# A Mamba-2 mixer with a routed low-rank FFN on one core: B/C convolution sums in two buffers, with one tap by ScalarE and GpSimd

## The reference

```
proj = xn @ in_proj_w.T            # gate, hBC, dt: 8192 + (8192 + 2*8*128) + 128 columns
hBC  = silu(causal_conv4(hBC) + conv_b)        # four taps along the tokens, per channel
dt   = softplus(dt + dt_bias);  A_dt = -exp(A_log) * dt
hs, B, C = split(hBC)              # 128 heads of 64; B and C: 8 groups of 128
Y_diag = ((C B^T) * exp(segsum(A_dt))) (hs*dt)     # inside chunks of 128 tokens
Y_off  = C @ (state carried over chunks) * exp(cumsum(A_dt))
y   = (Y_diag + Y_off + D*hs) * silu(gate), RMS-normalised over 8 groups of channels
out = x + y @ out_proj_w.T + (xn @ W.T + b) + lora_of_the_routed_rank(xn)
```

## Time and profile before

| | |
|---|---|
| median of 3 runs | 1671.41 us (1670.61 to 1672.05) |
| the profiled execution | 1669.55 us |
| its span, first to last instruction | 1667.8 us |
| TensorE matmuls busy | 1619.9 us (97%) |
| VectorE busy | 1387.0 us (83%) |
| ScalarE busy | 1262.7 us (76%) |
| GpSimd busy | 1149.4 us (69%) |
| mean granted TensorE clock | 0.994 |

### The profile page before, as it was taken

How to read it: one execution, slowest core, us unless ns; L and a number is a source line. 1 busy time by engine, 2 the same in 40 slices (tenths; PEclk the granted TensorE clock), 3 DMA queues, 4 the chain that set the end, 5 groups by cost and what they waited for, 6 DMA issues and landing times.

```text
span 1667.8 us, 28969 instructions
## 1 busy us (share of the span) xinstructions
PE 1619.9 (97%) x9662; PEld 1358.2 (81%) x9662; DVE 1387.0 (83%) x2342; ACT 1262.7 (76%) x2489; POOL 1149.4 (69%) x1472
## 2 busy tenths in 40 slices
PE   8889999999999999999997899999999999999998
PEld 6678888888888888888776788888888888888886
DVE  6778888888888888888887788888888888888887
ACT  3458888888888887888734687888888888888784
POOL 4227786777777677768652386877786777777684
PEclk9999999999999999999999999999999999999999
DMA  5134444444444444444312344444344444444431
GB/s 168 51 121 136 134 124 143 142 126 133 145 127 130 146 129 130 142 142 120 126 38 97 128 144 135 123 144 142 128 132 146 124 131 146 131 134 137 141 115 61
DMA packets 82309, 212.18 MB, mean 127 GB/s; under 512 B 11121, under 2 KB 27505, under 8 KB 81905
## 3 DMA queue, kind: packets, MB, share of 16 engines
q1 hardware_dynamic: 82160, 210.33, 40.2%
HBM read 207.14 MB, written 3.15 MB: 126 GB/s over the span
## 4 chain that ended last, share of the span: by engine, by line
PE 87%; DVE 8%; POOL 1%; issue 1%; ACT 1%; DMA 0%; POOLq 0%; DVEq 0%; ACTq 0%
PE bg L613 21%; PE bo L759 20%; PE bh L613 11%; PE bt L613 11%; PE by L812 8%; PE bg L832 5%; DVE cv L856 3%; PE bh L804 3%; PE bt L804 2%; PE bh L820 2%; PE bt L820 2%; ACT cv L319 1%; PE bo L670 1%; PE bg L738 1%; DVE ct L872 1%
## 5 line engine op out<-in xcount | busy, mean ns | idle before, releaser
L508 POOL TENSOR_TENSOR wl<-raw,wh 128x256 fp32r<-128x256 f32 x584 | 425.4, 760 | 138.4 <-ACT wh L315 138.4
L575 POOL TENSOR_TENSOR xl<-xg,xh 128x256 fp32r<-128x256 f32 x254 | 290.3, 1164 | 332.2 <-ACT xh L431 331.5
L332 ACT ACTIVATE mt<-cs_row,cs_tok 128x128 f32<-128x128 f32 x1024 | 324.8, 391 | 0.0
L589 POOL TENSOR_TENSOR wol<-raw_o,woh 128x256 fp32r<-128x256 f32 x256 | 181.6, 731 | 31.0 <-ACT woh L465 31.0
L1086 DVE TENSOR_TENSOR mt<-mt,gt 128x1024 f32<-128x1024 f32 x128 | 202.1, 1579 | 0.4 <-ACT mt L474 0.4
L759 PE MATMUL bo<-woh,xh 128*128 128x512 f32 x512 | 201.0, 393 | 0.9 <-POOL xl L575 0.9
L759 PE MATMUL bo<-wol,xh 128*128 128x512 f32 x512 | 200.4, 391 | 0.0
L759 PE MATMUL bo<-woh,xl 128*128 128x512 f32 x512 | 199.9, 391 | 0.0
L582 POOL TENSOR_TENSOR sqa<-sqa,sq 128x256 f32<-128x256 f32 x222 | 159.4, 738 | 0.9 <-ACT sq L448 0.9
L315 ACT ACTIVATE wh<-raw 128x1024 fp32r<-128x1024 f32 (+1 forms) x146 | 152.0, 1041 | 1.0 <-DMA raw<-in_w_dtag 1.0
L431 ACT ACTIVATE xh<-xg 128x512 fp32r<-128x512 f32 x128 | 81.0, 633 | 92.6 <-DVE xg L1066 92.6
(11 more groups left out here) (189 smaller groups left out, 3592.4 us busy)
## 6 DMA issues: line engine op xcount, KB each, us to landing
raw<-in_w_step SPq DMA_DIRECT2D x128, 512.0 KB, 3.5
cs_row<-cs_rows SPq DMA_DIRECT2D x128, 512.0 KB, 5.4
raw_o<-in_w_out SPq DMA_DIRECT2D x128, 256.0 KB, 4.1
ec_row<-ec_rows SPq DMA_DIRECT2D x256, 96.0 KB, 4.7
raw<-in_w_bc SPq DMA_DIRECT2D x16, 512.0 KB, 3.5
acc<-in_x SPq DMA_DIRECT2D x4, 512.0 KB, 5.7
cs_row<-in_w_ffn SPq DMA_DIRECT2D x2, 1024.0 KB, 6.8
out_dram<-acc SPq DMA_DIRECT2D x1, 1024.0 KB, 6.5
```

The source lines that it names most:

```text
L332: e = act.activation(mt[:, m % 2, h, chunk(j)], cs_row[:, m % 2, h, chunk(j)], ACT.Relu, bias=cs_tok[:, j, 2 * m + h:2 * m + h + 1], scale ...
L508: e = pool.tensor_tensor(wl[:, n % 2, cols], raw[:, n % 2, cols], wh[:, n % 2, cols].bitcast(F32), ALU.subtract)
L575: e = pool.tensor_tensor(xl[:, u, cols], xg[:, u, cols], xh[:, u, cols].bitcast(F32), ALU.subtract)
L589: e = pool.tensor_tensor(wol[:, 1 - u, cols], raw_o[:, 1 - u, cols], woh[:, 1 - u, cols].bitcast(F32), ALU.subtract)
```

## The change

It has four parts.

1. In the B/C stage the sums lie in two sets of buffers: `cv` for even groups, `sq` and `sqa` (free at that time) for odd ones (`conv_bc`). So the last tap of a group waits for the SiLU of two groups before.
2. Of the three taps that VectorE added, one goes to ScalarE and GpSimd: ScalarE writes the scaled, unshifted sum into `tap2[u]` (`two_taps`), and GpSimd adds it, shifted by one token, in two pieces of 256 and 255 columns (`add_tap`). VectorE adds the two others (`far_taps`) behind GpSimd's. In GpSimd's list the two `add_tap` of a group stand ahead of the low part of group `g + 2`, and all of them ahead of that of step 0.
3. VectorE masks the scores of group `g - 3` at the head of a group instead of between the taps of B and C, and waits for `scaled` only behind `soft_log` and `route`.
4. In the last batch's iteration m = 64 ScalarE's three instructions on the output weights and the copy of the last state stand ahead of `xh` and the square.

```diff
+        tap2 = mt[:, 0, 0], mt[:, 1, 1]
+        def conv_bc(g, u):
+            return cv[:, u, :] if g % 2 == 0 else (sq, sqa)[u]
...
+            def first_tap(b, g, u, src):
+                un = b * UNITS + 2 * g + u
+                if g != 1:
+                    act.wait_ge(v_h2, did(un - 2 if g == 0 else un - 4))
+                elif u == 0:
+                    act.wait_ge(p_sqa, squares(b - 1, STEPS - 1))
+                else:
+                    act.wait_ge(t_ss, did(b * GROUPS - 1))
+                act.activation(conv_bc(g, u)[:, :], src[:, :], ACT.Identity, bias=par_sb[:, un % UNITS, TAPS:TAPS + 1],
+                               scale=par_sb[:, un % UNITS, TAPS - 1:TAPS]).then_inc(a_tap, 1)
+            def two_taps(b, g, u, src):
+                un = b * UNITS + 2 * g + u
+                first_tap(b, g, u, src)
+                if g > 0:
+                    act.wait_ge(p_cv, did(bc_unit(b, g - 1, u)))
+                act.activation(tap2[u], src[:, :], ACT.Identity,
+                               scale=par_sb[:, un % UNITS, TAPS - 2:TAPS - 1]).then_inc(a_t2, 1)
...
-                    last_tap(b * UNITS + 2 * g, 0, bank_b[g % 2])
+                    two_taps(b, g, 0, bank_b[g % 2])
...
-                    last_tap(b * UNITS + 2 * g + 1, 1, bank_c[g % 2])
+                    two_taps(b, g, 1, bank_c[g % 2])
...
+                    ahead = m == STEPS and b + 1 == NB
+                    if ahead:
+                        weights_and_state()
                     if has(m - 2):
                         act.wait_ge(v_xg, did(n - 2))
...
-                    if has(m - 1):
-                        act.wait_ge(ld_rawo[1 - u], landed(n - 1))
...
+                    if has(m - 1) and not ahead:
+                        weights_and_state()
...
+            def add_tap(b, g, u):
+                pool.wait_ge(a_t2, did(bc_unit(b, g, u)))
+                for cols in (slice(1, 257), slice(257, L)):
+                    e = pool.tensor_tensor(conv_bc(g, u)[:, cols], conv_bc(g, u)[:, cols],
+                                           tap2[u][:, cols.start - 1:cols.stop - 1], ALU.add)
+                e.then_inc(p_cv, 1)
...
-                for g in range(2, GROUPS):
-                    split_lo(bc(b, g))
+                for g in range(GROUPS):
+                    for u in range(2):
+                        add_tap(b, g, u)
+                    if g + 2 < GROUPS:
+                        split_lo(bc(b, g + 2))
...
-                for k in range(1, TAPS):
-                    if k == 1:
-                        dve.wait_ge(a_tap, did(un))
+                for k in (2, 3):
+                    if k == 2:
+                        dve.wait_ge(p_cv, did(q))
...
-                    dve.wait_ge(scaled, SCALED)
                 soft_log(b)
                 route(b)
+                dve.wait_ge(scaled, SCALED)
                 for g in range(GROUPS):
                     un = b * UNITS + 2 * g
-                    taps_bc(b, g, 0, bank_b[g % 2])
-                    if g >= 1:
-                        silu_conv(un - 1, 1, bank_c[(g - 1) % 2], ct[:, g - 1, :])
                     if g >= 3:
                         mask_scores(b, g - 3)
-                    taps_bc(b, g, 1, bank_c[g % 2])
+                    far_taps(b, g, 0, bank_b[g % 2])
+                    if g >= 1:
+                        silu_conv(un - 1, conv_bc(g - 1, 1), bank_c[(g - 1) % 2], ct[:, g - 1, :])
+                    far_taps(b, g, 1, bank_c[g % 2])
```

More of the change, by code:

```diff
@@ L155, in mixer_kernel @@
         bank_b, bank_c, bank_t, bank_s = (bh, bt), (bg, by), (bh, bg), (bh, bt)
-        v_bc = sem("v_bc")
+        a_t2, p_cv, v_bc = sem("a_t2"), sem("p_cv"), sem("v_bc")
         ld_hp, ld_par, ld_wb, const_ok, scaled = (sem(n) for n in ("ld_hp", "ld_par", "ld_wb", "const_ok", "scaled"))
@@ L308, in _ @@
         def _(act):
-            start(act, (a_dr, a_tap, a_th, a_tg, a_rl, a_ex, a_s1, a_xh, a_sq, a_wh, a_wn, a_woh, a_bt))
+            start(act, (a_t2, a_dr, a_tap, a_th, a_tg, a_rl, a_ex, a_s1, a_xh, a_sq, a_wh, a_wn, a_woh, a_bt))
             act.wait_ge(ld_hp, 16)
@@ L324, in tanh_conv @@
                 act.activation(dst[:, :], cv[:, u, :], ACT.Tanh, scale=0.5).then_inc(a_th, 1)
+            def first_tap(b, g, u, src):
[15 more added lines that the diff above has]
+                               scale=par_sb[:, un % UNITS, TAPS - 2:TAPS - 1]).then_inc(a_t2, 1)
             def tanh_bc(b, g, u, dst):
-                act.wait_ge(v_bc, did(bc_unit(b, g, u), 3))
-                act.activation(dst[:, :], cv[:, u, :], ACT.Tanh, scale=0.5).then_inc(a_th, 1)
+                act.wait_ge(v_bc, did(bc_unit(b, g, u), 2))
+                act.activation(dst[:, :], conv_bc(g, u)[:, :], ACT.Tanh, scale=0.5).then_inc(a_th, 1)
             def rises(b, m, h):
@@ L427, in _, with weights_and_state @@
                         dt_parts(b + 1)
+                    def weights_and_state():
+                        act.wait_ge(ld_rawo[1 - u], landed(n - 1))
+                        act.activation(raw_o[:, 1 - u, :], raw_o[:, 1 - u, :], ACT.Identity,
+                                       scale=par_sb[:, 2 * GROUPS + m - 1, 6:7]).then_inc(a_wn, 1)
+                        act.wait_ge(a_wn, did(n - 1))
+                        act.wait_ge(t_out, did(n - 3))
+                        act.activation(woh[:, 1 - u, :], raw_o[:, 1 - u, :], ACT.Copy).then_inc(a_woh, 1)
+                        act.wait_ge(t_st, did(n - 1))
+                        act.wait_ge(t_off, did(n - 2))
+                        act.activation(S[:, 0, :], other[:, 0:P], ACT.Copy).then_inc(a_s1, 1)
+                    ahead = m == STEPS and b + 1 == NB
+                    if ahead:
+                        weights_and_state()
                     if has(m - 2):
@@ L480, in _ @@
         def _(pool):
-            start(pool, (p_acc, p_wl, p_wol, p_xl, p_sqa, p_rr))
+            start(pool, (p_cv, p_acc, p_wl, p_wol, p_xl, p_sqa, p_rr))
             pool.memset(ident[:, :], 0.0).then_inc(const_ok, 1)
@@ L847, in _, with far_taps @@
             start(dve, (v_bc, v_tap, v_h2, v_x, v_xd, v_m, v_s, v_y1, v_off, v_add, v_xg, v_sg, v_g, v_ms, v_acc))
-            def taps_bc(b, g, u, src):
+            def far_taps(b, g, u, src):
                 q, un = bc_unit(b, g, u), b * UNITS + 2 * g + u
-                for k in range(1, TAPS):
-                    if k == 1:
-                        dve.wait_ge(a_tap, did(un))
-                    else:
[L855 to L858, removed]
+                for k in (2, 3):
+                    if k == 2:
+                        dve.wait_ge(p_cv, did(q))
+                    else:
+                        dve.wait_ge(v_bc, did(q, 2, 1))
+                    dve.scalar_tensor_tensor(out=conv_bc(g, u)[:, k:], in0=src[:, 0:L - k],
+                                             scalar=par_sb[:, un % UNITS, TAPS - 1 - k:TAPS - k],
+                                             in1=conv_bc(g, u)[:, k:], op0=ALU.mult, op1=ALU.add).then_inc(v_bc, 1)
             def tap(n, un, u, src, k):
@@ L868, in tap, with silu_conv @@
                                          op0=ALU.mult, op1=ALU.add).then_inc(v_tap, 1)
-            def silu_conv(un, u, src, dst):
+            def silu_conv(un, conv, src, dst):
                 dve.wait_ge(a_th, did(un))
-                dve.scalar_tensor_tensor(out=dst, in0=src[:, :], scalar=1.0, in1=cv[:, u, :],
+                dve.scalar_tensor_tensor(out=dst, in0=src[:, :], scalar=1.0, in1=conv[:, :],
                                          op0=ALU.add, op1=ALU.mult).then_inc(v_h2, 1)
@@ L1027, in _ @@
                     dve.wait_ge(const_ok, CONST)
-                    dve.wait_ge(scaled, SCALED)
                 soft_log(b)
                 route(b)
+                dve.wait_ge(scaled, SCALED)
                 for g in range(GROUPS):
                     un = b * UNITS + 2 * g
-                    taps_bc(b, g, 0, bank_b[g % 2])
-                    if g >= 1:
-                        silu_conv(un - 1, 1, bank_c[(g - 1) % 2], ct[:, g - 1, :])
                     if g >= 3:
                         mask_scores(b, g - 3)
-                    taps_bc(b, g, 1, bank_c[g % 2])
+                    far_taps(b, g, 0, bank_b[g % 2])
+                    if g >= 1:
+                        silu_conv(un - 1, conv_bc(g - 1, 1), bank_c[(g - 1) % 2], ct[:, g - 1, :])
+                    far_taps(b, g, 1, bank_c[g % 2])
                     if g >= 2:
                         dve.wait_ge(t_bt, did(b * GROUPS + g - 2))
-                    silu_conv(un, 0, bank_b[g % 2], h2[:, g % 2, :])
+                    silu_conv(un, conv_bc(g, 0), bank_b[g % 2], h2[:, g % 2, :])
                     if g == 1:
@@ L1046, in _ @@
                         decays_to_end(b)
-                silu_conv(b * UNITS + 2 * GROUPS - 1, 1, bank_c[(GROUPS - 1) % 2], ct[:, GROUPS - 1, :])
```

(3 more changed lines are left out.)

## The result

| | before | after |
|---|---|---|
| median of 4 runs each, us | 1671.01 | 1648.24 (1646.76 to 1649.77) |
| ratio | | 0.9863, 95% interval 0.9846 to 0.9880 |
| profiled execution's span, us | 1667.8 | 1646.2 |
| VectorE busy, us | 1387.0 | 1367.2 |
| ScalarE busy, us | 1262.7 | 1281.6 |

The kernel is 1.4% faster: 22.9 us by the ratio, 21.6 by the two spans. The forecast was 20.9 us.

What follows compares the result with a forecast made beforehand. TensorE, busy 97% of the span, was taken as the bound, so only its waits and slow clock could pay. Gains of 10.3 (batch 0), 7.9 (batch 1) and 2.7 (end) sum to 20.9 us: 1650.5 us, range 1645 to 1656.5.

Steps and rivals of the forecast that it cites:

- The walk of batch 0: Batch 0's B/C stage, traced from router to step 0: transposes at 37.6, scores of group 1 at 59.1, step 0 at 94.3.
- the stand before step 0: Once per batch TensorE waits 4.8 us for step 0's low half, queued on GpSimd behind the last tap of C.
- slow clock in step 0 of batch 0: TensorE's clock falls behind the 4.8 us wait before step 0, charged 2.7 us; the same charge in batch 1.
- small waits of steps 0 and 1, batch 0: A TensorE wait of 0.37 us in step 0 goes because VectorE has caught up: 0.4 us gained.
- batch 1, step 0 earlier still by: Batch 1's step 0 starts at 919.4 instead of 929.56, 10.2 us earlier, before 2.7 is charged for the clock.
- the end: In the tail, copying the last state first lets VectorE go on at 1651.5 instead of 1654.24: 2.7 us gained.
- The router beside GpSimd: In batch 0 the router's tiny instructions, now beside GpSimd's first taps and a split, cost 2.7 us more.
- B: Rival: clock doesn't fall behind the 4.8 wait before step 0, or that wait is mostly hidden; 5.4 more gained, 1645.1; chance 0.10.
- C: Rival: GpSimd's adds cost about 1.16 each, or the clock falls at 37.6 too; 5.4 less gained, 1655.9; chance 0.17.
- D: Rival: GpSimd bounds the B/C stage at about 1.2 us a piece, period 9.6; slower, 1677; chance 0.04.
- GpSimd off the path: In the B/C stage GpSimd's 5.7 us a period stays below TensorE's 6.78, so its slower add costs nothing.
- VectorE's 4.8 us a period: In the B/C stage VectorE, with one tap less per sum, needs 4.8 us a period, below TensorE's 6.78.

## Why the prediction was right

**The walk of batch 0 held.** Forecast: router's transposes at 37.6, C of group 3 at 56.4, scores of group 1 at 59.1, step 0 at 94.3. Measured 37.19, 56.42, 59.27 and 93.58. The router was 0.4 early and the walk from it to the scores of group 1 took 22.1 for 21.5, which nearly cancel. The periods are 6.7 (forecast 6.78), and the stand before step 0 is 4.45 (4.8) in both batches. The tap by ScalarE takes 0.68, as forecast, and GpSimd's adds 1.41 to 1.44 a pair against the 1.48 taken from the steps' sums. The pairs beside VectorE's decays take up to 2.45; they delayed nothing.

**Part by part, by the starts of TensorE's instructions:**

| | forecast | measured |
|---|---|---|
| batch 0, step 0 earlier by | 12.6 | 106.89 - 93.58 = 13.3 |
| slow clock in step 0 of batch 0 | -2.7 | 4.45 - 2.84 for 12 matmuls = -1.6 |
| small waits of steps 0 and 1, batch 0 | +0.4 | +0.6 |
| between the B/C stages | 0 | -2.0 |
| batch 1, step 0 earlier still by | 10.2 | 10.6 |
| slow clock in step 0 of batch 1 | -2.7 | 5.15 - 2.84 = -2.3 |
| small waits, batch 1 | +0.4 | +0.6 |
| the steps of batch 1 | 0 | -0.3 |
| the end | +2.7 | +2.7 |
| sum | 20.9 | 21.6, as by the spans |

That the sum came within 0.7 us is in part luck: the terms that came out better than forecast add 3.0 us, and the two that were put at nothing take 2.3 of them away again. The measured gain at the end has two parts. TensorE's waits are 2.0 shorter, and in the kernel before the granted clock was 0.50 behind the wait of 3.41, where in the change it stays at 1.00.

**What was mis-sized.** The router beside GpSimd: I charged 2.7; the copy, two maxima and three masked products took 3.0 more than without GpSimd, but the four larger products behind them took 2.19 in place of 2.94, so 2.3 net.

The middle: nothing was forecast there, and 2.0 were lost. In the profiled execution of the change twelve output matmuls at the turn of the batches took 821.97 - 817.52 = 4.45 us at a granted clock of about half, where they took 2.86 before: 1.6. The waits ahead of them (1.27 and 0.43) are the same as before. Of the ten experiments nine ran through that place at full clock, and one (the changed kernel with the mask back) did not, so nothing ties this fall to the change; without it the gain would have been some 1.6 more. The other 0.4 lies in the 64 steps of batch 0; its cause stays open, as does that of the 0.3 in the steps of batch 1. The forecast of the clock behind the stand was right in kind in both batches and too large by 1.1 in the first and by 0.4 in the second.

**The rivals.** The clock fell behind both stands, so B did not happen. Its 5.4 us are less than half of what it is worth to have neither the stand nor the slow clock: with low half and mask ahead the kernel is 12.5 us faster than the change by the ratios. C and D wanted GpSimd's pieces at about 1.15 us or more; the median of the adds was 0.73 to 0.74. D's mechanism, GpSimd as the bound, would have needed no idle time on it: its timeline above shows 0.53 of idle time before B's add and 1.30 before C's in a steady group, and 2.54 before the last group.

**What the argument undervalued.** The prediction puts GpSimd off the path, so that the slower add costs nothing, and charges the moved tap only for its places in the queues. It took VectorE's 4.8 us a period as part of why TensorE isn't held. The experiments show that 6.3 would have done as well, so the change is right as a whole and one part of it is a loss: by ratio, 0.9863 with the moved tap and 0.9784 without. The prediction's own terms said as much. They charge the moved tap with 4.8 + 2.7 us in each batch and with 2.7 at the router, and none of them credits it with a gain; the sum without it was never drawn up. The Trainium skill's advice (GPSIMD Engine Reference, section "Engine selection"), to keep elementwise sums of two inputs on VectorE, agrees with that outcome. The add is slower on GpSimd here too, 1.42 a pair against 0.75 for VectorE's tap, but in the steady groups that costs nothing. What costs is what it delays elsewhere: 1.42 of wait for the router, and 4.45 twice before step 0, the latter with what the clock takes.

The lock on the shared port pair that the Trainium skill describes (SBUF - State Buffer, "Who interferes with whom") agrees with the rows of the router above: four-element instructions with two SBUF inputs, and the copy, take 0.65 to 0.74 beside GpSimd, about a GpSimd piece, and 0.16 to 0.18 without it, while the taps of this stage, with one input from PSUM, stay at 0.74 to 0.75 in every kernel. The prediction told this lock as one against two SBUF inputs only; that section of the Trainium skill names copies as well, and the copy's 0.74 bears it out.

## What to carry to other kernels

When an engine waits for a small instruction, look first at where it stands in its engine's order: a mask moved by one place, with a second buffer, was worth about 20 us more than with either one missing, so edits that break two parallel chains have to be tried together. Before work is moved to a less busy engine, list what stands behind it in that queue at the end of the stage: here the next stage's weights. And after the bound has moved to another engine, try the offload again without: it may have become a pure cost.

## What the runs showed of the hardware

TensorE's clock after a wait was not a fixed thing. It fell to the lower level behind every wait of 3.27 us and more that the traces show, and behind those of 2.86 and 2.6 (step 0 with the low half ahead, window 96 to 98 at 0.50). Behind 3.09 us it stayed up once and fell once in the B/C stage of batch 0 of one execution (the kernel with the mask back), and fell again in batch 1:

```profile
96.00:98.00 2.00, 1.36 (x12) 1.00 0.00 0
98.00:100.00 2.00, 2.00 (x10) 1.00 0.00 0
106.00:108.00 2.00, 1.32 (x6) 0.50 0.00 0
108.00:110.00 2.00, 2.00 (x9) 0.50 0.00 0
```
(columns as in the earlier trace rows; the waits end at 96.64 and 106.68.) Behind the 3.0 to 3.1 us with which every run begins it was at 1.00 in all twelve traces. Behind the waits of 1.8 before scores it never fell. Yet behind a wait of the same length at the start of the run it fell in seven of eleven traces (in the twelfth that wait was 2.37, and it fell too), and the matmuls behind it started at about half speed. It stayed up there in the two traces that are compared above, so this is not in their difference. Timelines of TensorE in the kernel before and in the one with the tap back on VectorE:

```profile
13.30 1.17 PE L613 MATMUL bh<-xTh,wh 128*128 128x512 f32 x4 [1.83 <-DVE xTl L933]
```
```profile
13.29 2.04 PE L652 MATMUL bh<-xTh,wh 128*128 128x512 f32 x4 [1.82 <-DVE xTl L972]
```
At the turn of the batches it fell in two of the twelve executions behind waits of 1.27 and about 0.43, and stayed up in the ten others behind the same. So the length of the last wait alone doesn't settle whether the clock falls. The falls sized above cost 1.6 and 2.3 us. That may be why runs of one kernel differ by as much (the change's four runs span 3.0 us), but there is one trace for each kernel, so it is not shown.
